# A fused decoder layer with mixture-of-experts routing: GpSimd's four scattered row writes of a step, one at a time between its masks

## The reference, cut to what matters

```
x = x + attn(layernorm(x))          # softmax over att * tril(k=-1), 16 heads
x = x + cross_attn(layernorm(x), ctx)
scores = softmax(layernorm(x) @ gate_w.T); top 2 of scores + gate_bias
x = x + sum_e mlp_e(layernorm(x)) * weight_e + mlp_shared(layernorm(x))
```

## Time and profile before

| what | us |
| --- | --- |
| median of 3 runs | 706.56 (706.29 to 707.81) |
| span of the profiled execution | 730.5 |
| PE busy | 651.7 (89%) |
| POOL busy | 458.5 (63%) |
| ACT busy | 472.1 (65%) |
| DVE busy | 429.3 (59%) |
| the 64 indirect writes of sorted rows on POOL (line 2226) | 64.4 |

### The profile page before, as it was taken

One profiled execution on the slowest core, in us unless ns is written; L12 is line 12 of the kernel. 1 busy time (PEld: TensorE's weight loads), 2 busy tenths in 40 slices (PEclk: granted clock), 3 DMA queues, 4 the chain that ended last, 5 costly groups with the idle time before them and its releaser, 6 DMA issues.

```text
span 730.5 us, 17333 instructions
## 1 busy us (share of the span) xinstructions
PE 651.7 (89%) x5530; PEld 494.9 (68%) x5530; DVE 429.3 (59%) x1168; ACT 472.1 (65%) x1106; POOL 458.5 (63%) x778
## 2 busy tenths in 40 slices
PE   5887899999999999999999999999996798989894
PEld 2344567767677776776867768668785677778674
DVE  2356556867768677686777867746555332322237
ACT  3344687877878878678777886777862354645540
POOL 4345474787877878678786786676655155555560
PEclk9769999999999999999999999999998999999998
DMA  4824526245352453525426245122204232222119
GB/s 137 227 46 123 115 83 188 60 132 147 65 173 48 145 146 78 160 46 147 147 62 171 48 149 146 38 107 92 61 26 108 59 86 81 77 75 68 37 56 309
DMA packets 65111, 77.95 MB, mean 107 GB/s; under 512 B 9314, under 2 KB 50679, under 8 KB 64896
## 3 DMA queue, kind: packets, MB, share of 16 engines
q1 hardware_dynamic: 59884, 67.70, 33.6%
q0 software_dynamic: 4352, 8.47, 3.9%
q10 hardware_dynamic: 788, 0.69, 0.4%
HBM read 54.30 MB, written 22.64 MB: 105 GB/s over the span
## 4 chain that ended last, share of the span: by engine, by line
PE 66%; issue 9%; DVE 6%; ACT 5%; DMA 5%; POOL 4%; SPq 3%; another core or an unknown queue 2%; ACTq 0%; POOLq 0%; DVEq 0%
PE banks L1061 10%; PE banks L1023 7%; PE banks L327 7%; PE banks L800 7%; PE banks L1043 5%; PE banks L349 3%; PE banks L840 3%; PE banks L810 3%; PE banks L808 2%; PE banks L338 2%; PE banks L862 1%; DMA k_stack<-parts 1%; DMA qst<-q_parts 1%; PE banks L843 1%
## 5 line engine op out<-in xcount | busy, mean ns | idle before, releaser
L1476 ACT ACTIVATE prob<-banks 128x512 f32<-128x512 f32 x192 | 114.8, 602 | 63.1 <-PE banks L803 60.7
L2201 POOL TENSOR_SCALAR_AFFINE_SELECT prob<-prob 128x256 f32<-128x256 f32 (+1 forms) x192 | 92.3, 500 | 56.6 <-ACT prob L1476 55.8
L1752 DVE TENSOR_REDUCE mx<-banks 128x2 f32<-128x512 f32 x128 | 87.1, 681 | 42.4 <-PE banks L810 39.2
L1061 PE MATMUL banks<-info,xprobT 128*128 128x128 f32 (+1 forms) x832 | 103.9, 275 | 1.0 <-issue 0.8
L1061 PEld LDWEIGHTS banks<-info,xprobT 128*128 128x128 f32 (+1 forms) x832 | 100.4, 192 | 2.8 <-issue 1.2
L800 PE MATMUL banks<-kst,qst 48*128 48x128 bf16 (+1 forms) x512 | 76.5, 251 | 18.7 <-issue 5.4
L1783 DVE TENSOR_REDUCE xmax<-banks 128x1 f32<-128x896 f32 x64 | 63.0, 985 | 27.7 <-PE banks L1023 18.4
L2226 POOL DMA_INDIRECT sorted_rows<-row,place x64 | 64.4, 1005 | 23.0 <-issue 18.6
L510 DVE TENSOR_TENSOR xprobT<-banks,xprob 128x512 f32<-128x512 f32 x36 | 24.9, 692 | 88.4 <-ACT xprob L419 66.0
L803 PE MATMUL banks<-qst,kst 51*128 51x128 bf16 (+1 forms) x512 | 75.1, 249 | 0.1
L1748 DVE TENSOR_REDUCE mx<-banks 128x4 f32<-128x512 f32 x64 | 44.1, 690 | 45.5 <-PE banks L808 39.1
(11 more groups left out here) (196 smaller groups left out, 1636.9 us busy)
## 6 DMA issues: line engine op xcount, KB each, us to landing
infoT<-in_ctxT SPq DMA_DIRECT2D x16, 800.5 KB, 5.5
info<-in_ctx SPq DMA_DIRECT2D x16, 448.0 KB, 3.8
kst<-k_stack SPq DMA_DIRECT2D x31, 192.0 KB
info<-in_ctx SPq DMA_DIRECT2D x16, 320.0 KB
q_parts<-parts SPq DMA_DIRECT2D x31, 96.0 KB, 2.3
k_stack<-parts SPq DMA_DIRECT2D x31, 96.0 KB, 2.3
qst<-q_parts SPq DMA_DIRECT2D x31, 96.0 KB
infoT<-sorted_rows SPq DMA_DIRECT2D x36, 65.0 KB
```

What stands on the lines that cost most here:

```text
L1061: mm = pe.matmul(ps[:, V_BANK, u * P:(u + 1) * P], lhsT=xprobT[hf][0:w, m - blocks[0], :], rhs=info[0:w, m, :], start=(m == blocks[0]), st ...
L1476: act.activation(prob[n % 2][:, kind * 512:(kind + 1) * 512], ps[:, gamma_bank_of(b, v), :], ACT.Exp, scale=SCALE).then_inc(s["p_exp"], 1)
L1752: dve.tensor_reduce(mx[:, 1, h:h + 2, 0], bank.rearrange("p (c n) -> p c n", c=2), AX.X, ALU.max).then_inc(s["alpha_max"], 1)
L2201: pool.affine_select(out=w, in_=w, compare_op=ALU.is_gt, fill=0.0, base=0, pattern=[[0, 4 if kind == 2 else 2], [1, P]], channel_multiplie ...
```

## The change

`send_rows` is cut into `send_row(l, n)` for n = 0 to 3. The waits stay ahead of the first of the four. In a step the four are no longer issued back to back: the first keeps its place behind mask 2, the second stands behind mask 3, the third behind mask 4, and the fourth behind mask 5 and `deviation2`, directly ahead of `split_rest`. Transfers, sizes, indices and semaphores are the same. `finish()` still calls `send_rows`, so the last four sequences are sent as before. The new order is in force for i = 4 to 15, twelve steps.

```diff
+            def send_row(l, n):
+
+                if not live(l):
+                    return
+                if n == 0:
+                    pool.wait_ge(s["placed"], l + 1)
+                    pool.wait_ge(s["row_x"], 2 * l + 2)
+                    pool.wait_ge(s["weigh"], 3 * l + 3)
+                    if l == B - 1:
+                        pool.wait_ge(s["blank_out"], 16 * E)
+                t, c = n // TOPK, n % TOPK
+                pool.indirect_dma_start(dsort, bass.IndirectOffsetOnAxis(ap=place[:, t, c:c + 1], axis=0), row[:, c, t, :], None,
+                                        bounds_check=SORTED - 1, oob_is_err=False).then_inc(s["sent"], 16)
+
             def send_rows(l):
...
+                for n in range(T * TOPK):
+                    send_row(l, n)
...
                 masked(i, 2)
-                send_rows(l)
+                send_row(l, 0)
                 masked(i, 3)
+                send_row(l, 1)
                 masked(i, 4)
+                send_row(l, 2)
                 masked(i, 5)
                 deviation2(g)
+                send_row(l, 3)
                 split_rest(f + 1, 0)
```

More of the change, by code:

```diff
@@ L2213, in row_inputs, with send_rows @@
                 pool.tensor_copy(row[:, :, :, D + 1].bitcast(I32), home[:, :, 2 * l:2 * l + T]).then_inc(s["row_x"], 1)
-            def send_rows(l):
+            def send_row(l, n):
                 if not live(l):
                     return
[L2219 to L2227, removed]
+                if n == 0:
[7 more added lines that the diff above has]
+                                        bounds_check=SORTED - 1, oob_is_err=False).then_inc(s["sent"], 16)
+            def send_rows(l):
+                for n in range(T * TOPK):
+                    send_row(l, n)
             def residual(j):
```

## The result

The changed kernel takes 719.48 us (median of 6 runs, 716.71 to 723.48) against 707.18 us (704.32 to 708.76) for the kernel before on the same chip: a ratio of 1.016 with a 95% interval of 1.012 to 1.0199, 12.3 us. I had forecast 715.8 us in a range of 708 to 720. The direction, the mechanism and the place were right. The price of the send behind `deviation2` was too small, and the loss is spread over the run otherwise than I had it.

What follows compares the result with a forecast made beforehand. TensorE's list was taken to set the step, with under 1 us idle. Losses of 5.7 us (six steps), 2.5 (steps 5, 8), 0.95 (step 15) and 0.1 (steps 4, 13, 14) make 9.2; 706.56 + 9.2 = 715.8 us, range 708 to 720.

Steps and rivals of the forecast that it cites:

- The order argument: GpSimd's list: sends hid under waits before; one now stands behind the last wait, so the order can only finish later.
- The price of the fourth send: Between `deviation2` and `qk_r` on GpSimd: the send delays `qk_r` and everything down to `xdiff` by 1.27 us.
- first path: `qk_r` to ScalarE's cast to TensorE's scores 9: 0.37 us slack at the cast in step 7, 0.82 us late at TensorE.
- The two paths lead to the same engine one after the other, so the larger counts: Both delays reach TensorE; a step loses only the larger, 0.95 us in step 7, 1.27 us where there is no slack.
- second path: `xdiff` through ScalarE and VectorE's `q_lo` to TensorE's cross scores: 0.32 us slack in step 7, TensorE 0.95 us late.
- The sum: Losses over steps 4 to 15: 5.7 + 2.5 + 0.95 + 0.1 = 9.2 us.
- The 23.9 us: Median shorter than the profiled span by this much, placed by no row; the 9.2 us were carried over to the median unchanged.
- Slower, but by less: Rival: unprofiled, GpSimd has more slack, say 0.7 us a step; loss 5.0 us, 711.5 us; chance 0.15.
- not slower: Rival: GpSimd's unprofiled slack absorbs the send; 706.6 us (no change, 0.08) or down to 705.0 us (gain, 0.07); chance 0.15.
- relief of the `qst` loads: TensorE's waits for `qst` loads: spreading the writes could return nothing to 1.6 us; none was taken in the forecast.
- A send meets VectorE's copy: Rival: all nine sends behind `deviation2` wait out VectorE's 0.69 us copy; 6.2 us more, 722.0 us; chance 0.04.
- Alternation is dear: Rival: sends alternating with masks cost 2.72 us each, 6 us in each of twelve steps, about 780 us; chance 0.03.

Runs made afterwards that it cites:

- the repetition: The kernel before, unaltered, run and profiled a second time: median 707.66 us, ratio 0.9999; profiled span 707.6 us.
- the edits: On the changed kernel, ScalarE's cast of `qk_r` behind exponential 8 (719.42 us), `xdiff` ahead of mask 6 (717.69 us), or the two together (715.49 us).
- Relieving the first: Changed kernel with ScalarE's cast of `qk_r` moved behind exponential 8: 719.42 us, ratio 1.0118 to the kernel before.
- relieving the second: Changed kernel with GpSimd's `xdiff` moved ahead of mask 6: 717.69 us, ratio 1.0104 to the kernel before.
- second profiles: Each kernel run and profiled once more without edit: median 707.66 us for the kernel before, 720.33 us for the changed one.
- both edits: Changed kernel with ScalarE's cast behind exponential 8 and `xdiff` ahead of mask 6: 715.49 us, ratio 1.0073 to the kernel before.

## Why the prediction came out as it did

**What bounds the kernel: right.** TensorE's list sets the step, and all of the added 0.77 us is idle time of TensorE.

**The order argument: right, with one sentence too strong.** What it named is in the trace of the changed kernel, but for the idle time ahead of mask 5, which stands ahead of mask 4 (0.24 us): the idle time of 0.48 us ahead of `deviation2`, its start right behind the variance, one send between it and `qk_r`, the cast's wait, and the wait of scores 9. The run with only the fourth send moved gives the whole loss, the one without it 0.27%. That no order of the same pieces finishes them earlier than the one before holds only where GpSimd is free when the variance comes; in the repetition it isn't, and two sends ahead of mask 0 bring `deviation2` forward by 0.4 to 0.6 us.

**The price of the fourth send: the term that was mis-sized.** I took 1.27 us, from a send behind a mask or behind another send. Behind the 0.19 us operation that ends `deviation2` it took 0.56 us of idle and 1.08 us of work, and `qk_r` started 3.23 us behind the first operation of `deviation2` instead of 1.52 us: 1.71 us. I bounded this price from above with the first send of the run (2.72 us) and took the lower bound, a row of a send in another place. Behind the 1.16 us `qk_r` the send had only 0.17 us of idle.

**The slack and the first path: right as a mechanism.** 1.71 us less the 0.37 us of slack is 1.34 us, and the cast does start 4.54 us behind the variance instead of 3.18 us, 1.36 us later. ScalarE's idle time is only 1.10 us, since ScalarE itself came 0.25 us later. TensorE waited 1.06 us, where I had 0.82 us; 0.77 us reached step 7, where I had 0.95 us.

**"The two paths lead to the same engine one after the other, so the larger counts": right, and it is what the edits showed.** Relieving the first leaves a step of 30.92 us, relieving the second 30.67 us, of 30.98 us, and relieving most of both 30.26 us; before it was 29.89 us. So the second path alone costs 1.03 us and the first alone 0.78 us, near the 0.95 and 0.82 us that I had, and the second is the larger, as forecast. In the changed kernel it hides behind the first, which holds up ScalarE and TensorE ahead of it, so that `xc` waits only 0.35 us. That these two sizes came out near is in part luck: the send cost 0.44 us more than I took, and in the repetition GpSimd won back some 0.57 us at `deviation2` that I hadn't seen.

**The sum.** 9.2 us forecast, 12.3 us measured. The spans of the second profiles of the two kernels are 10.8 us apart (718.4 and 707.6 us). Divided at the first sends of the steps:

| stretch | forecast us | second profiles us |
| --- | --- | --- |
| ahead of step 4 | 0 | 0.8 |
| step 4 | almost 0 | 0.5 |
| steps 5 to 12 | 8.2 | 6.5 |
| steps 13 and 14 | almost 0 | 0.6 |
| from step 15 on | 0.95 | 2.4 |

So the dearer send doesn't by itself explain why the total was over the forecast. The eight steps in the middle cost less than forecast, 6.5 us here and 3.5 us between the first profiles, where the kernel before has long steps of its own (31.29 us in step 9 of its first profile, 32.27 us in step 11 of the second); against its shorter steps each lost 1.0 to 1.1 us. The ends cost more. In step 4 the stretch from the first send to `qk_r` took 8.41 us instead of 8.03 us, again the dearer send, and TensorE waited 2.00 us; it had waited 0.78 us in the earlier trace rows and 1.54 us in the repetition. In steps 14 and 15 there is no `qk_r` and so no first path (the slack at the cast that I gave step 14 doesn't exist). In step 15 `xc` waited 1.75 us, and TensorE 0.85 us for `q` and 0.57 us for `q_lo` behind it, 1.42 us against 0.95 us forecast. The remaining 1.5 us between profiles and medians is within the spread of the runs and has no cause shown.

**The 23.9 us: right to leave alone.** Between the two profiles of the kernel before 19.7 of 22.9 us lie behind the last send.

**The rivals.** *Slower, but by less* and *not slower* both rested on unseen slack on GpSimd outside the profile; the repetition shows less slack, not more. The relief of the `qst` loads that a gain needed isn't there either: TensorE waited 4.9 and 5.5 us for them in the two profiles of the changed kernel, 4.4 and 6.3 us in those of the kernel before. *A send meets VectorE's copy*: in step 4 of the changed kernel the two ran side by side.

```profile
163.71 1.09 POOL L2226 DMA_INDIRECT sorted_rows<-row,place  x1 [0.56 <-issue]
163.71 0.69 DVE L1840 COPY oT<-banks 128x512 f32<-128x512 f32 x1
```

The send took 1.09 us there and 1.07 to 1.09 us behind every `deviation2`, with a copy beside it or not, and the longest of all, 1252 ns, stood behind a wait for a transfer in `finish()`. So none waited a copy of 0.69 us out. By the Trainium skill (SBUF — State Buffer, the "DVE blocks DMA" trap), VectorE in a two-port mode locks GpSimd out, which then can't write descriptors; no run here shows that, and since this copy reads from PSUM, it may not be such a case. *Alternation is dear*: a send directly behind a mask has 0.17 to 0.33 us of idle ahead of it, and the run that alternates with no send behind `deviation2` lost 0.27%.

## What to carry to other kernels

A write that an engine issues for nobody in a hurry belongs where that engine waits anyway; the same write behind the last wait of its list delays everything that follows. Count what stands behind the inserted instruction, reader by reader, until the list next idles: two late products hide each other, and mending one shows little. Take the price of an issue from one that stands in the same kind of place, and where there is none, carry the upper bound through the sum as well.

## What was not expected of the hardware

- The idle time ahead of an indirect write depends on what precedes it. In the changed kernel it was 0.17 us behind a 0.64 us mask, 0.33 us behind a 0.40 us mask that had just been released, and 0.56 us behind the 0.19 us end of `deviation2`; in other runs it was 0.17 us behind the 1.16 us `qk_r` and 0.30 us behind another send. The length of the predecessor alone doesn't decide: the first send of step 7 stands behind a 0.40 us mask too, and has 0.18 us. What does, no run tells.
- The first indirect write of the run had 1.50 us of idle ahead of it in the kernel before and 1.74 us in the changed one, and took 1.22 us. With two sends ahead of mask 0 it still took 1.22 us, but had only 0.18 us of idle ahead of it. So that idle time doesn't come with being the first; what it is stays open.
- TensorE's granted clock fell behind an idle time of 2.00 us once and stayed at 2.4 GHz behind the same one in another execution of the same program. With two sends behind `deviation2` it fell behind 2.32 us in six of the steps 5 to 12 and stayed behind 2.04 and 2.32 us in the other two. Shorter ones did it too: 1.24 us in step 14 with both edits, and 1.31 us in step 11 of the repetition of the kernel before, the step of 32.27 us, where the granted clock from 369 to 372 us was 0.66. Behind the 1.06 us of steps 5 to 12 in the changed kernel it stayed at 1.00. A wait of TensorE is thus a risk as well as a cost, from 1.24 us on in these traces, and what decides was not found.
